# One expert layer of a deep kernel, dense over all experts, rewritten as a routed layer over tiles of slots

## The chip, the cores and the metric

The kernel runs on one core of a Trainium2 chip. The metric is the device time of one execution in microseconds, as the median over several runs. The kernel is one program that computes a network of four blocks, each an attention-like part and a feed-forward part; the change touches one of the eight parts, the feed-forward part of the third block.

## The reference

The part in question routes each of 2048 tokens (128 features) to one of 8 experts, an expert being two linear maps with 512 hidden features between them. In the reference all experts are computed for all tokens, and a mask keeps the chosen one:

```
B, S, D = (8, 1024, 128); H = 512; O = 128; E = 8; TOP_K = 1
xf = x.reshape(-1, d)
router_logits = xf @ Wr + br
topk_logits, topk_idx = jax.lax.top_k(router_logits, TOP_K)
topk_gates = jax.nn.softmax(topk_logits, axis=1)
for k in range(TOP_K):
    idx_k = topk_idx[:, k]
    gate_k = topk_gates[:, k:k + 1]
    for e in range(E):
        h = jax.nn.relu(xf @ W1[e] + b1[e])
        oe = h @ W2[e] + b2[e]
        mask = (idx_k == e)[:, None]
        out = out + jnp.where(mask, gate_k * oe, 0.0)
```

With one expert per token the softmax runs over one value, so the gate is 1. The layer's input is the normalised stream, and its output is added to the stream H.

## The kernel before

The program is written as a row of stages, each a block with one instruction stream per engine; a barrier of all engines closes a block. The part in question is called with the name "m2" and is made of five of them. `normalise` (m2n) writes XT, features by tokens. `route_softmax` (m2r) makes the logits (L229, L243), takes the largest (L246, L249), builds a gate per token and expert and stores the gates to DRAM; at the same time XT is split into a high and a low part (XR) and the weights of expert 0 are split on GpSimd (L379, L381). `relu_experts` (m2x) is the expert stage; `add_turned` (m2a) turns the result back and adds it to H (L169, L177). The same functions serve another layer, m1, with 16 experts.

Every product is made of three matmuls of reduced-precision parts (`product`, L306 to L308): high x high, low x high, high x low. So each factor must be split first. In `relu_experts` a step s is one expert e, one group g of 512 tokens, and one chunk c of 128 of the 512 hidden features: 8 x 4 x 4 = 128 steps. Per step TensorE makes the first product (`first`, into one of four PSUM banks `ph`) and, three steps behind it (LAG), the second (`second`, summed over the four chunks into `py`). ScalarE applies the relu with bias (L493) and, for even steps, makes the high part HS (L500); VectorE makes the high part of odd steps (L528), the low part of all (L532), and the gating and adding per group (L540, L549). The weights of the next expert are rounded by ScalarE (L506) and their low part is made by VectorE (L553), once in 16 steps. SyncE loads weights and gate rows, an expert or more ahead.

Two other places of the program matter for reading the change. `choose_tokens` gathers 2048 rows of 512 bytes from DRAM in 16 indirect DMAs on GpSimd, each with one row number per partition (L1247). `route_grouped` counts tokens per expert in a chain of 15 dependent additions (L997).

The order of the work on each engine is the order in which it is written; nothing reorders it, and a wait holds up all that stands behind it on its engine or queue.

## Time and profile before

| | us |
|---|---|
| median of 3 runs | 3247.32 |
| lowest and highest run | 3238.9, 3250.64 |
| the profiled execution, its own time | 3243.43 |
| its span, first to last instruction | 3241.6 |
| TensorE busy (share of the span) | 2544.6 (78%) |
| VectorE busy | 2352.4 (73%) |
| ScalarE busy | 1327.5 (41%) |
| GpSimd busy | 1419.5 (44%) |
| mean granted TensorE clock | 0.892 |

The rows are of that one execution. The busy shares are averages over stages with different limits, so for one stage they say little. Times within the trace are counted from the first instruction; the m2 part fills the stretch from about 2621 to 2854 us.

### The profile page before, as it was taken

The numbers are of one execution on the slowest core, as the hardware profiler recorded it, in microseconds if no ns is written. First come the engines' busy times: TensorE is split into PE (matmuls) and PEld (weight loads), VectorE is DVE, ScalarE is ACT, GpSimd is POOL, SyncE is SP. The second block draws the span as 40 slices with busy tenths as digits, with TensorE's granted clock in tenths as the row PEclk, the third lists the DMA queues.
The fourth block names the chain that finished last, engine by engine and source line by source line (L and its number), as shares of the span: only waits on it lengthen the run. The fifth ranks groups of instructions, "written<-read, shape, count | busy, mean of one in ns | idle before, by whom it ended". The sixth has DMA issues, their size and how long they took to land. (4 is left out here: it accounts for less than half of the span.)

```text
span 3241.6 us, 29207 instructions
## 1 busy us (share of the span) xinstructions
PE 2544.6 (78%) x8955; PEld 1510.7 (47%) x8955; DVE 2352.4 (73%) x3437; ACT 1327.5 (41%) x2109; POOL 1419.5 (44%) x897
## 2 busy tenths in 40 slices
PE   1778777677787772999857979479999659969599
PEld 0323222332332331666534837357777437733366
DVE  5699799759988976555557485658888548859566
ACT  2644444254454431222253343147776326730222
POOL 1499789649978971111123516110000310017266
PEclk9899889889999985999878989779999859979799
DMA  5155065116505410565300000022120011100021
GB/s 138 34 121 115 13 131 111 36 23 127 118 23 119 105 54 17 134 139 139 92 17 10 17 0 0 5 74 76 62 79 27 6 53 63 43 12 18 12 81 65
DMA packets 86604, 203.35 MB, mean 63 GB/s; under 512 B 12816, under 2 KB 25184, under 8 KB 77920
## 3 DMA queue, kind: packets, MB, share of 16 engines
q1 hardware_dynamic: 85952, 200.63, 24.6%
q8 instruction: 64, 1.05, 0.1%
q0 software_dynamic: 512, 1.05, 0.1%
q14 instruction: 76, 0.62, 0.1%
HBM read 198.76 MB, written 2.88 MB: 62 GB/s over the span
## 5 line engine op out<-in xcount | busy, mean ns | idle before, releaser
L532 DVE TENSOR_TENSOR m1x_HS<-m1x_R,m1x_HS 128x512 fp32r<-128x512 f32 x256 | 175.8, 691 | 69.2 <-ACT m1x_HS L500 64.9
L493 ACT ACTIVATE m1x_R<-m1x_ph,m1s_W 128x512 f32<-128x512 f32 x256 | 176.3, 689 | 107.2 <-PE m1x_ph L308 106.5
L1337 POOL TENSOR_TENSOR t2x_KM<-t2x_KT,t2x_HM 128x2048 f32<-128x2048 f32 x8 | 28.8, 3603 | 432.7 <-ACT t2x_KT L1410 416.0
L1688 POOL TENSOR_TENSOR t3xs_QH<-t3xs_HS,t3xa_Q 128x512 f32<-128x512 f32 x64 | 81.0, 1266 | 287.9 <-DVE t3xs_HS L1672 287.9
L829 DVE TENSOR_TENSOR m0x_T<-m0x_S,m0x_pb 128x512 f32<-128x512 f32 x128 | 88.1, 689 | 131.3 <-PE m0x_pb L308 131.2
L815 ACT ACTIVATE m0x_S<-m0x_pa 128x512 f32<-128x512 f32 x128 | 76.5, 598 | 214.2 <-PE m0x_pa L308 214.2
L2117 PE MATMUL t0x1fs_acc<-t0x1fs_HC,g_ident 128*128 128x512 f32 x256 | 133.6, 654 | 38.6 <-POOL t0x1fs_HC L2198 38.5
L2117 PE MATMUL t0x0fs_acc<-t0x0fs_HC,g_ident 128*128 128x512 f32 x256 | 133.2, 651 | 38.3 <-POOL t0x0fs_HC L2198 38.2
L2117 PE MATMUL t0x1bs_acc<-t0x1bs_HC,g_ident 128*128 128x512 f32 x256 | 131.2, 641 | 39.3 <-POOL t0x1bs_HC L2198 39.2
L2117 PE MATMUL t0x0bs_acc<-t0x0bs_HC,g_ident 128*128 128x512 f32 x256 | 130.2, 639 | 35.7 <-POOL t0x0bs_HC L2198 35.6
L2198 POOL TENSOR_TENSOR t0x1bs_HC<-t0x1bs_HS,t0x1bs_CB 128x1024 f32<-128x1024 f32 x64 | 149.1, 2360 | 10.7 <-DMA t0x1bs_CB<-t0x1b_bc_rows 4.2
L2198 POOL TENSOR_TENSOR t0x0bs_HC<-t0x0bs_HS,t0x0bs_CB 128x1024 f32<-128x1024 f32 x64 | 149.2, 2363 | 10.0 <-DMA t0x0bs_CB<-t0x0b_bc_rows 3.8
L2198 POOL TENSOR_TENSOR t0x1fs_HC<-t0x1fs_HS,t0x1fs_CB 128x1024 f32<-128x1024 f32 x64 | 148.5, 2343 | 7.0 <-DMA t0x1fs_CB<-t0x1f_bc_rows 5.2
L2198 POOL TENSOR_TENSOR t0x0fs_HC<-t0x0fs_HS,t0x0fs_CB 128x1024 f32<-128x1024 f32 x64 | 148.7, 2350 | 5.4 <-DMA t0x0fs_CB<-t0x0f_bc_rows 4.0
L332 POOL TENSOR_TENSOR m0s_WR<-m0s_W,m0s_ZERO 128x256 fp32r<-128x256 f32 x32 | 26.8, 838 | 259.6 <-DMA m0s_W<-in_L_units 259.4
L794 PE MATMUL m0x_acc<-m0x_HF,m0s_W 128*128 128x512 f32 x256 | 131.5, 595 | 3.8 <-DVE m0x_HF L838 3.8
L532 DVE TENSOR_TENSOR m2x_HS<-m2x_R,m2x_HS 128x512 fp32r<-128x512 f32 x128 | 88.0, 692 | 44.0 <-ACT m2x_HS L500 41.8
L493 ACT ACTIVATE m2x_R<-m2x_ph,m2s_W 128x512 f32<-128x512 f32 x128 | 88.2, 689 | 54.0 <-PE m2x_ph L308 53.6
L634 POOL TENSOR_TENSOR m3x_HF<-m3x_T,m3x_GS 128x512 f32<-128x512 f32 x64 | 81.7, 1280 | 58.0 <-DVE m3x_T L706 55.7
L306 PE MATMUL m1x_py<-m1x_HS,m1s_WR 128*128 128x512 f32 x256 | 103.3, 403 | 1.4 <-DVE m1x_HS L532 1.3
L306 PE MATMUL m0x_pa<-m0s_XR,m0s_WR 128*128 128x512 f32 x128 | 101.8, 795 | 1.8 <-PEq L890 1.8
L306 PE MATMUL m1x_ph<-m1s_XR,m1s_WR 128*128 128x512 f32 x256 | 102.3, 400 | 0.0
(915 smaller groups left out, 7637.6 us busy)
## 6 DMA issues: line engine op xcount, KB each, us to landing
m0x_GS<-m_gate_rows SPq DMA_DIRECT2D x64, 512.0 KB, 6.6
t0x0fs_CB<-t0x0f_bc_rows SPq DMA_DIRECT2D x32, 512.0 KB, 6.3
t0x0bs_CB<-t0x0b_bc_rows SPq DMA_DIRECT2D x32, 512.0 KB, 6.5
t0x1fs_CB<-t0x1f_bc_rows SPq DMA_DIRECT2D x32, 512.0 KB, 6.4
t0x1bs_CB<-t0x1b_bc_rows SPq DMA_DIRECT2D x32, 512.0 KB, 6.6
m1x_GS<-m_gate_rows SPq DMA_DIRECT2D x16, 1024.0 KB, 4.7
m1s_W<-in_L_w SPq DMA_DIRECT2D x16, 514.0 KB, 3.3
m2x_GS<-m_gate_rows SPq DMA_DIRECT2D x8, 1024.0 KB, 4.7
```

Of the source, the lines that this page charges most:

```text
L306: pe.matmul(out, lhsT[0], rhs[0], start=start, stop=False, skip_group_check=True)
L332: pool.tensor_tensor(self.WR[:, j, 0, :], self.W[:, j, 0:self.cut], self.ZERO[:, :], ALU.add).then_inc(self.rounded, 1)
L493: a.activation(R[:, s % 4, :], ph[s % 4][:, :], ACT.Relu, bias=W[:, e % RAW, weights.cut + c:weights.cut + c + 1]).then_inc(relu_ready, 1)
L532: v.tensor_tensor(HS[:, s % 4, 1, :], R[:, s % 4, :], HS[:, s % 4, 0, :].bitcast(F32), ALU.subtract).then_inc(low_made, 1)
L634: nc.gpsimd.tensor_tensor(HF[:, s % 3, :], T2[:, s % 2, :], GS[:, u // 2 % 2, tokens(g)], ALU.mult).then_inc(gated, 1)
L794: pe.matmul(acc[g][:, :], W[:, u % RAW, 2 * P:3 * P], HF[:, s % 3, :], start=(u == 0), stop=(u == UNITS - 1), skip_group_check=True).then_ ...
L815: nc.scalar.activation(S[:, s % 2, :], pa[s % 2][:, :], ACT.Silu).then_inc(s_ready, 1)
L829: v.tensor_tensor(T2[:, s % 2, :], S[:, s % 2, :], pb[s % 2][:, :], ALU.mult).then_inc(t_ready, 1)
L1337: nc.gpsimd.tensor_tensor(KM[:, i % 2, :, :], keys, spread(HM[:, :], W), ALU.mult).then_inc(km_made, 1)
L1688: nc.gpsimd.tensor_tensor(QH[:, s % 4, :], HS[:, s % 4, :], Q[:, c], ALU.mult).then_inc(read, 1)
L2117: mm = pe.matmul(acc[:, dh, :], ident[:, :], HC[:, m % 3, dh, :], start=False, stop=False, skip_group_check=True)
L2198: nc.gpsimd.tensor_tensor(HC[:, m % 3, :, :], HS[:, m % 5, :, :], rows, ALU.mult).then_inc(hc_made, 1)
```

## The change

The call of `relu_layer` for m2 is replaced by two new functions. `route_sparse` finds each token's expert and gives it a slot: the tokens of an expert stand one after another, each expert's slots begin at a multiple of 512, and 11 tiles of 512 slots hold every possible distribution. The 16 tiles of normalised rows are scattered into a DRAM array of 11 x 512 rows, cleared before. `sparse_experts` then works on the tiles: it loads 512 rows, turns them on TensorE, splits them (high part on ScalarE, low part on VectorE), runs 4 chunks as before, adds the second bias, turns the result back, and stores it. At the end GpSimd gathers each token's row, and VectorE multiplies by the gate and adds it to H. The weights of a tile's expert are gathered by row number, four tiles' worth up front; the later ones by GpSimd between its splits of the low parts, which it now makes. The first bias and the second stand in the weight rows (1029 columns). All 11 tiles are computed, full or empty. The router's matmuls and the normalisation stay as they were.

```
+def route_sparse(nc, name, XT, XN, ident, iota, earlier, pick, w_router, b_router, w12, E, out):
...
+            @block.sync
+            def _(sp):
+                sp.dma_start(wr[:, :], w_router[:, :]).then_inc(loaded, 16)
+                sp.dma_start(br[:, :], b_router.partition_broadcast(P)).then_inc(loaded, 16)
+                sp.wait_ge(blanked, 1)
+                for q in range(GROUPS):
+                    part = slot_rows[q * P * NT:(q + 1) * P * NT, :].rearrange("(p a) d -> p (a d)", a=NT)
+                    sp.dma_start(part, blank[:, :]).then_inc(cleared, 16)
...
+            @block.vector
...
+                for t in range(1, TILES):
+                    link(v.tensor_tensor(ahead[:, t, :], ahead[:, t - 1, :], inall[:, t - 1, :], ALU.add))
...
+            @block.gpsimd
+            def _(pool):
+                nc.gpsimd.memset(blank[:, :], 0.0).then_inc(blanked, 1)
+                pool.wait_ge(weight_row_ready, 1)
+                for j in range(len(w_loaded)):
+                    pool.indirect_dma_start(W[:, j, :], None, w12,
+                                            bass.IndirectOffsetOnAxis(ap=weight_row[:, j:j + 1], axis=0)).then_inc(w_loaded[j], 16)
+                pool.wait_ge(slot_ready, 1)
+                pool.wait_ge(cleared, 16 * GROUPS)
+                for t in range(TILES):
+                    pool.indirect_dma_start(slot_rows, bass.IndirectOffsetOnAxis(ap=slot[:, t:t + 1], axis=0),
+                                            XN[:, t, :], None).then_inc(scattered, 16)
...
+def sparse_experts(nc, name, H, ident, w12, out_rows, r):
...
+            @block.sync
+            def _(sp):
+                sp.wait_ge(scattered, 16 * TILES)
+                for j in range(3):
+                    sp.dma_start(XG[:, j, :, :], rows(slot_rows, j)).then_inc(x_loaded[j], 16)
+                for j in range(NT):
+                    sp.wait_ge(yt_read, j + 1)
+                    sp.dma_start(rows(out_rows, j), YT[:, j % 2, :, :]).then_inc(y_stored[j % 2], 16)
+                    if j + 3 < NT:
+                        sp.wait_ge(x_turned, j + 1)
+                        sp.dma_start(XG[:, j % 3, :, :], rows(slot_rows, j + 3)).then_inc(x_loaded[j % 3], 16)
...
+            @block.tensor
...
+                for s in range(STEPS):
+                    j, c = s // C, s % C
+                    if c == 0 and j + 1 < NT:
+                        turn_in(j + 1)
+                    if s + LAG < STEPS:
+                        first(s + LAG)
+                    second(s)
+                    if c == 1 and j:
+                        turn_out(j - 1)
+                turn_out(NT - 1)
...
+            @block.scalar
...
+                def round_w(j):
+                    act.wait_ge(w_loaded[j % RAW], 16 * (j // RAW + 1))
+                    if j >= 2:
+                        act.wait_ge(summed, (j - 1) * C)
+                    a.activation(WR[:, j % 2, 0, :], W[:, j % RAW, 0:CUT], ACT.Copy).then_inc(w_high, 1)
...
+                round_x(0)
+                for s in range(STEPS + 1):
+                    j, c = s // C, s % C
+                    if s < STEPS:
+                        relu(s)
+                    if s and (s - 1) % 2 == 0:
+                        high(s - 1)
+                    if s < STEPS and c == 0 and j + 1 < NT:
+                        round_w(j + 1)
+                        round_x(j + 1)
+                    if c == 3 and j:
+                        read(j - 1)
+                read(NT - 1)
...
+            @block.vector
...
+                split_x(0)
+                for s in range(STEPS):
+                    j, c = s // C, s % C
+                    low(s)
+                    if c == 0 and j + 1 < NT:
+                        split_x(j + 1)
+                    if c == 3 and j:
+                        copy_y(j - 1)
...
-        relu_layer("m2", 8, 1, "L2_ffn_Wr", "L2_ffn_br", "L2_w12", "L2_ffn_b2")
+        with Stage(nc, "m2s") as s:
+            NT, E = 11, 8
+            XN = s.sb("XN", [P, TILES, P])
+            normalise(nc, "m2n", H, XT, ident, XN)
...
+            route_sparse(nc, "m2r", XT, XN, ident, iota, consts["earlier"], consts["pick"], ins["L2_ffn_Wr"],
+                         ins["L2_ffn_br"], ins["L2_w12"], E, r)
+            sparse_experts(nc, "m2x", H, ident, ins["L2_w12"], out_rows, r)
```

ScalarE's row in the expert stage before, where the first chunks are followed by the rounding of the next expert's weights (R is the relu's output, HS the high part, WR the split weights, OT the sum):

```order
L510 ACTIVATE m2s_OT<-m2x_py 128x512 x4
L493 ACTIVATE m2x_R<-m2x_ph,m2s_W 128x512 x2
L500 ACTIVATE m2x_HS<-m2x_R 128x512
L493 ACTIVATE m2x_R<-m2x_ph,m2s_W 128x512 x2
L500 ACTIVATE m2x_HS<-m2x_R 128x512
L493 ACTIVATE m2x_R<-m2x_ph,m2s_W 128x512 x2
L500 ACTIVATE m2x_HS<-m2x_R 128x512
L493 ACTIVATE m2x_R<-m2x_ph,m2s_W 128x512
L506 ACTIVATE m2s_WR<-m2s_W 128x1024
```

The same engine in the changed program, one tile from its first relu to the next tile's (XR is the split x, Y the second product with its bias):

```order
L863 ACTIVATE m2x_R<-m2x_ph,m2s_W 128x512
L850 ACTIVATE m2s_WR<-m2s_W 128x1024
L856 ACTIVATE m2x_XR<-m2x_px 128x512
L863 ACTIVATE m2x_R<-m2x_ph,m2s_W 128x512
L870 ACTIVATE m2x_HS<-m2x_R 128x512
L863 ACTIVATE m2x_R<-m2x_ph,m2s_W 128x512 x2
L870 ACTIVATE m2x_HS<-m2x_R 128x512
L876 ACTIVATE m2x_Y<-m2x_py,m2s_W 128x512
L863 ACTIVATE m2x_R<-m2x_ph,m2s_W 128x512
```

The rounding of weights stood once in 16 steps; now it stands once in 4, with the rounding of x behind it, both between a tile's first relu and the first high part.

SyncE's queue before, through the m2 stages (GS are the gate rows, W the weights):

```order
L212 DMA m2r_wr<-in_L_ffn_Wr 128x8
L213 DMA m2r_br<-in_L_ffn_br 128x8
L369 DMA m2s_W<-in_L_w 128x1028 x3
L218 DMA m_gate_rows<-m2s_gateF 8x512 x4
L434 DMA m2x_B<-in_L_ffn_b 8x128
L439 DMA m2x_GS<-m_gate_rows 128x2048
L369 DMA m2s_W<-in_L_w 128x1028
```

and in the changed program (XG are the loaded rows of a tile, YT the turned result):

```order
L622 DMA m2r_wr<-in_L_ffn_Wr 128x8
L623 DMA m2r_br<-in_L_ffn_br 128x8
L627 DMA m_slot_rows<-m2r_blank 128x1408 x4
L764 DMA m2x_XG<-m_slot_rows 128x512 x3
L767 DMA m_out_rows<-m2x_YT 128x512
L770 DMA m2x_XG<-m_slot_rows 128x512
L767 DMA m_out_rows<-m2x_YT 128x512
```

The weights have left this queue, and each load of x now stands behind a store.

GpSimd before did the first splits and was then idle until the next block; in the changed program it issues the indirect DMAs (slot holds a row number per token, weight_row one per partition and tile):

```order
L705 MEMSET m2r_blank 128x1408
L708 DMA m2s_W<-in_L_w,m2s_weight_row 128x1029 x4
L713 DMA m_slot_rows<-m2s_XN,m2s_slot 5632x128 x16
L776 TENSOR_TENSOR m2s_WR<-m2s_W,m2s_WR 128x1024 x2
L782 DMA m2s_W<-in_L_w,m2s_weight_row 128x1029
L776 TENSOR_TENSOR m2s_WR<-m2s_W,m2s_WR 128x1024
```

After the last tile another 16 indirect DMAs (L788) gather the results.

## Rows read from the trace of the kernel before

**Rows 1.** Windows: the expert stage; us, busy us (instructions) per engine, clock, DMA

```profile
core 0: us, PE busy (x) PEld busy (x) DVE busy (x) ACT busy (x) POOL busy (x), PEclk, DMA share, GB/s
2662.00:2848.00 186.00, 183.98 (x768) 144.46 (x768) 154.72 (x262) 127.95 (x200) 0.00 (x0) 0.99 0.13 46
```

**Rows 2.** Waits in 2664 to 2848: who for whom, us in total, times, longest

```profile
ACT m2x_R L493 <- PE m2x_ph L308: 53.6, 113, 1.0
...
PEld m2x_py L306 <- DVE m2x_HS L532: 7.3, 16, 1.1
```

**Rows 3.** Timeline, routing of m2: start us, duration us, engine, line, operation

```profile
2642.03 0.29 DVE L243 TENSOR_TENSOR m2r_logits<-m2r_pl,m2r_br 128x128 f32<-128x128 f32 x1 [10.51 <-PE m2r_pl L229]
...
2645.88 0.23 DVE L251 CAST m2r_wheref<-m2r_where 128x128 f32<-128x128 uint32 x1
```

**Rows 4.** Timeline, end of m2

```profile
2849.13 3.65 PE L169 MATMUL m2a_turned<-g_ident,m2s_OT 128*128 128x128 f32 x16 [1.77 <-PEq L431]
...
2852.82 0.69 DVE L177 TENSOR_TENSOR g_H<-g_H,m2a_turned 128x512 f32<-128x512 f32 x1 [0.16 <-PE m2a_turned L169]
```

**Rows 5.** Timeline, the counting chain of layer m0

```profile
1282.34 3.80 DVE L997 TENSOR_TENSOR m0r_ahead<-m0r_ahead,m0r_inall 128x64 f32<-128x64 f32 x15
```

**Rows 6.** Timeline, the gathers of choose_tokens, first and last of 16

```profile
43.14 0.17 DVE L1228 CAST tok_index<-tok_spreadrows 128x16 uint32<-128x16 f32 x1 [0.70 <-PE tok_spreadrows L1240]
43.61 1.15 POOL L1247 DMA_INDIRECT g_H<-in_x,tok_index  x1 [43.19 <-DVE tok_index L1228]
...
62.54 0.94 POOL L1247 DMA_INDIRECT g_H<-in_x,tok_index  x1 [0.30 <-issue]
65.19 0.87 DVE L1232 BATCH_NORM_STATS2 t0m_stats<-g_H 128x6 f32<-128x128 f32 x4 [4.19 <-DMA g_H<-in_x,tok_index]
```

**Rows 7.** DMA issues: count, KB each, us from issue to landing

```profile
m1s_W<-in_L_w SPq DMA_DIRECT2D x16, 514.0 KB, 3.3
...
t0x0fs_BB<-t0x0f_bc_rows SPq DMA_DIRECT2D x21, 256.0 KB, 3.6
...
g_H<-in_x,tok_index POOLq DMA_INDIRECT x16, 2.5
t0x0i_WI<-in_L_attn_in SPq DMA_DIRECT2D x1, 256.0 KB, 2.5
...
t0x0b_bc_rows<-t0x0bp_BCF SPq DMA_DIRECT2D x1, 256.0 KB, 2.6
```

**Rows 8.** Groups by line, 2621 to 2866: busy us, mean ns, idle before

```profile
L506 ACT ACTIVATE m2s_WR<-m2s_W 128x1024 fp32r<-128x1024 f32 x7 | 7.4, 1056 | 0.0
...
L147 ACT ACTIVATE g_XT<-m2n_turned 128x512 f32<-128x512 f32 x4 | 2.4, 598 | 3.1 <-PE m2n_turned L154 3.1
...
L381 POOL TENSOR_TENSOR m2s_WR<-m2s_W,m2s_WR 128x1024 fp32r<-128x1024 f32 x1 | 2.3, 2342 | 0.1
```

**Rows 9.** Timeline, first products of the expert stage

```profile
2663.77 0.63 PE L307 MATMUL m2x_ph<-m2s_XR,m2s_WR 128*128 128x512 f32 x1
...
2664.20 0.63 PE L308 MATMUL m2x_ph<-m2s_XR,m2s_WR 128*128 128x512 f32 x1
```

**Rows 10.** Timeline, near the stage's end: VectorE, then ScalarE

```profile
2841.21 0.69 DVE L532 TENSOR_TENSOR m2x_HS<-m2x_R,m2x_HS 128x512 fp32r<-128x512 f32 x1 [0.42 <-ACT m2x_HS L500]
2841.82 0.42 DVE L528 TENSOR_SCALAR m2x_HS<-m2x_R 128x512 fp32r<-128x512 f32 x1
2842.27 0.69 DVE L532 TENSOR_TENSOR m2x_HS<-m2x_R,m2x_HS 128x512 fp32r<-128x512 f32 x1
...
2842.75 0.69 ACT L493 ACTIVATE m2x_R<-m2x_ph,m2s_W 128x512 f32<-128x512 f32 x1 [0.70 <-PE m2x_ph L308]
2843.34 0.62 ACT L500 ACTIVATE m2x_HS<-m2x_R 128x512 fp32r<-128x512 f32 x1
```

**Rows 11.** Windows of 2 us in the scan layer; columns as in rows 1

```profile
444.00:446.00 2.00, 0.16 (x1) 0.00 (x0) 2.00 (x2) 1.31 (x2) 2.00 (x1) 1.00 0.39 83
...
454.00:456.00 2.00, 0.37 (x1) 0.38 (x2) 2.00 (x2) 1.13 (x3) 2.00 (x2) 0.89 0.50 156
456.00:458.00 2.00, 2.00 (x3) 0.80 (x3) 1.97 (x2) 1.20 (x2) 2.00 (x2) 0.50 0.94 137
```

More of the change, by code:

```diff
@@ L2902, in build @@
         recycle(nc)
-        relu_layer("m2", 8, 1, "L2_ffn_Wr", "L2_ffn_br", "L2_w12", "L2_ffn_b2")
+        with Stage(nc, "m2s") as s:
+            NT, E = 11, 8
+            XN = s.sb("XN", [P, TILES, P])
+            normalise(nc, "m2n", H, XT, ident, XN)
+            r = dict(tiles=NT, gate=s.sb("gate", [P, TILES]), slot=s.sb("slot", [P, TILES], U32),
+                     weight_row=s.sb("weight_row", [P, NT], U32), W=s.sb("W", [P, 4, ins["L2_w12"].shape[-1]]),
+                     WR=s.sb("WR", [P, 2, 2, 8 * P], F32R), w_high=s.sem("w_high"), w_split=s.sem("w_split"),
+                     w_loaded=[s.sem(f"w_loaded{j}") for j in range(4)], scattered=s.sem("scattered"),
+                     slot_rows=nc.dram_tensor("m2_slot_rows", (NT * GROUP, P), F32, kind="Internal").ap())
+            out_rows = nc.dram_tensor("m2_out_rows", (NT * GROUP, P), F32, kind="Internal").ap()
+            route_sparse(nc, "m2r", XT, XN, ident, iota, consts["earlier"], consts["pick"], ins["L2_ffn_Wr"],
+                         ins["L2_ffn_br"], ins["L2_w12"], E, r)
+            sparse_experts(nc, "m2x", H, ident, ins["L2_w12"], out_rows, r)
         recycle(nc)
@@ L2932, in lay_out @@
     d = {"x": a["x"]}
-    for n in ("L1_ffn_router_w", "L1_ffn_router_b", "L1_ffn_b2", "L2_ffn_Wr", "L2_ffn_br", "L2_ffn_b2"):
+    for n in ("L1_ffn_router_w", "L1_ffn_router_b", "L1_ffn_b2", "L2_ffn_Wr", "L2_ffn_br"):
         d[n] = a[n]
@@ L2939, in lay_out @@
                                         b1.reshape(E, 4, P).transpose(0, 2, 1)], axis=2)
+    d["L2_w12"] = np.concatenate([d["L2_w12"], a["L2_ffn_b2"][:, :, None]], axis=2).reshape(8 * P, -1)
     d["L0_tok_W"], d["L0_tok_b"] = a["L0_tok_W"], a["L0_tok_b"]
@@ L2949, in lay_out @@
     d["c_pick"] = np.concatenate([blocks % 8 == np.arange(8), blocks // 8 == np.arange(TILES), blocks * P,
-                                  np.zeros((P, TILES - 1))], axis=1).astype(np.float32)
+                                  blocks, np.zeros((P, TILES - 2))], axis=1).astype(np.float32)
     m = {n: a["L0_attn_" + n] for n in ("in_proj_w", "conv_w", "conv_b", "xproj_w", "dtproj_w", "dtproj_b", "A_log",
```

250 lines of the change are left out of this document (added).

## The prediction

> **What bounds the kernel now.** I read three views. The whole program is long and only the layer called m2 changes, so I cut that out with the windows view. From 2662 to 2848 us TensorE is busy 184.0 of 186 us at a granted clock of 0.99, with VectorE at 154.7 and ScalarE at 128.0 [rows 1]: the expert stage runs at TensorE's pace. The waits say the same: ScalarE waits 53.6 us for TensorE's products, TensorE's weight port only 7.3 us for VectorE [rows 2]. The same window gives the pace: 768 matmuls of 512 columns in 186 us, 0.24 us each; six of them make a step (3 for the first layer, 3 for the second), so 1.4 us, and 128 steps make the 180 us. The routing ahead of it starts its VectorE part at 2642.03 [rows 3], and the last addition to H ends at 2852.82 + 0.69 = 2853.51 [rows 4]. What precedes 2642.03 (normalise, router weights, router matmuls) and what follows 2853.51 is the same in both programs. So the sum is made on one stretch: 211.5 us now.
>
> **The change, part by part.** It replaces 8 experts x 4 groups x 4 chunks = 128 steps by 11 tiles x 4 = 44 steps. It adds a slot computation on VectorE, 4 weight gathers and 16 scatters on GpSimd, a trip through DRAM for the rows, per tile two turns on TensorE and an x split, and 16 gathers at the end. At TensorE's pace alone 84 steps less would save 118 us. I walk the new path instead.
>
> *1. Slot computation.* The same 3.9 us from the logits to the cast of the indices [rows 3], then the chosen mask (about 0.3) and two matmuls (0.5). Then 15 chained additions: the same loop in layer m0 takes 3.80 us for 15 of 64 columns [rows 5], 0.25 each; with 8 columns I take 0.2, 2.9 in all. Ten more small links of 0.2 to 0.28 give the weight rows. Sum 9.8: 2651.8. The slots are 2 us later, behind the weight gathers, so they cost nothing.
>
> *2. GpSimd's indirect DMAs.* The trace has 16 gathers of the same shape (128 rows of 512 B): 43.61 for the first, 62.54 for the last, 15 starts later, so 1.26 us each; the last data is used at 65.19, 2.65 after its issue [rows 6], and the landing is given as 2.5 [rows 7]. Here 4 weight gathers (rows of 4.1 KB) and 16 scatters stand in one row: 0.3 to start (43.31 to 43.61 there) + 19 x 1.25 + 2.5 = 26.6: the rows lie in DRAM at 2678.4. The clearing of the slots (four stores, 2.9 MB) is queued over 20 us ahead of the first scatter, and 0.5 MB lands in 3.3 [rows 7]: hidden. No row shows a scatter or a gather of 4.1 KB rows; below, I take no less than 1.25, above twice that, and choose 1.25 since the count of rows is the same.
>
> *3. Fill.* Load of x 2.8 (256 KB: 2.5 alone, 3.6 beside others [rows 7]), turn at half clock 1.1 (16 of them take 3.65 [rows 4]), rounding 0.65 [rows 8], subtraction 0.75, then three first products at half clock of 1.28 each (0.43 x 3 [rows 9]) = 9.2: 2687.6, where the turn for tile 1 begins. Neither the 26.6 nor the 9.2 has a counterpart now.
>
> *4. One middle tile, from the moment L at which its next x has landed.* An engine starts its next instruction about 0.1 before the last one's reported end: ScalarE 0.59 after a relu of 0.69; VectorE 0.61 after a subtraction of 0.69, 0.45 after a cast of 0.42 [rows 10]. ScalarE's order is fixed: relu, round w (1.06 [rows 8]), round x, relu, high, relu, relu, high, read. Turn in to L+0.5; round x 0.55 to 1.15; relu from 1.05; high 1.65 to 2.27; VectorE: low 2.3, x subtraction 2.9, cast 3.5, low 3.95, low 4.6, cast 5.2, low 5.65, and only then the copy of the turned y, 6.25 to 6.9. TensorE meanwhile turns, does one first product (to 1.2), **waits for the low part until 3.05**, and ends the tile's eighth product at L+8.7. Its own work is 24 x 0.24 + 8 turns (1.0) = 6.8, so about 2 us of idleness per tile come from ScalarE's queue: the high part of the very chunk that TensorE wants stands behind round w and round x. The weight split on GpSimd (2.34 [rows 8]) ends by about L+3.5, ahead of its use at 3.75.
>
> *5. Who waits behind the store.* SyncE's order is: wait for the copied y of tile j, store it, and only then issue the load of x for tile j+3. The copy that comes at L+6.9 therefore releases the x that is wanted at L+8.7. Store issue 0.5, load landing 2.5 (alone) to 3.6 (beside other traffic) [rows 7]; I take 3.3, since a 256 KB store is right ahead of it. That is L+10.7: x is late by 2 us, and the loop copy, store, load, turn, copy sets the period, not TensorE. It holds for x 3 to 10.
>
> *6. Clock.* Per tile TensorE now has two gaps of about 2 us. Rows of the scan layer: after a gap of the same kind at 444 the clock stayed at 1.00; after the one at 454 it fell to 0.50 [rows 11]. So gaps of this length stand at the border between the two levels (1.2 and 2.4 GHz). I add 0.3 us per tile as a mean: period 11.0.
> The Trainium skill, TensorE: Matmul & The Clock Gate, section "HAM oscillation — how this bites in real kernels", speaks against this change: waits between short bursts take the clock down each time, so that every burst begins at half rate. By that rule every tile pays; by the row at 444 none does. What this would be is a rival below, worked out from rows.
>
> *7. Sum.* 2687.6; tile 0 without load stall or turn out 8.4: 2696.0; tile 1 10.7; tiles 2 to 8 7 x 11.0 = 77.0; tile 9 without a load to wait for at its end 8.7; tile 10 has no rounding in front of it and runs at TensorE's pace, 4.2: 2796.6. Read, turn out, copy 2.0; store 2.6 [rows 7]: 2801.2. Gathers 0.3 + 15 x 1.25 + 2.5 = 21.5; four additions of 0.35 with little overlap 1.3: **2824.0**. Against 2853.5 that is 29.5 us less. The profiled execution took 3243.4 us by its own time (span 3241.6), so 3213.9; the median of the runs is 3.9 above it: **3218**.
>
> **Weights.** The gather of tile n is issued once the y that used its buffer is read, about 15 us before the rounding wants it; 514 KB land in 3.3 [rows 7]. Hidden with 10 us to spare; if it were not, each of 7 tiles would pay its lateness.
>
> **The rivals.**
> *A, x is not late (0.15).* If store and load do not disturb each other and the copy comes earlier than walked, the period is that of step 4 with the weight rounding starting at the tile's beginning, about 9.1. For it: WI landed in 2.5. Against: even 2.5 gives L+9.9. Gain 29.5 + 8 x 1.9 = 45: 3203.
> *B, TensorE's pace holds (0.05).* 6.8 us per tile: tiles 1 to 8 save about 4.2 more each and tiles 0 and 9 about 1.7, gain 29.5 + 37 = 66: 3181. Against it stands ScalarE's order.
> *C, half clock in every tile (0.18).* First and second products cost 1.28 instead of 0.70. Between L and the copy lie the turn, two seconds, one first and the turn out: these push the copy from 6.9 to 9.3, the period from 10.7 to 13.1, 2.1 above the one in the sum. Gain 29.5 - 8 x 2.1 - 4 for the other tiles = 9: 3239. For it: two gaps with one short burst between them come close to what stood ahead of the fall at 454 [rows 11]. Against: the rest of the tile is one long burst.
> *D, slower than before (dearer DMAs 0.12, of which 0.07 dear enough to lose).* 36 indirect DMAs are on the path, each with GpSimd's issue time. At 1.25 they cost 45 us of the 182 that the new path takes. From 1.25 + 29.5/36 = 2.07 us each the change loses; at 2.5, twice the row, it is 3218 + 36 x 1.25 = 3263. For it: a scatter writes DRAM and the weight rows are 8 times longer; against: the time is per row index, and all 16 seen cost the same 1.25 but the first. The Trainium skill, DMA: Bandwidth & Descriptors, section "Bandwidth", advises batches of 1 MiB and calls transfers under 64 KB descriptor-bound, which these 32 transfers are at the edge of.
> *E, no effect.* Not possible: 84 of 128 steps do go.
>
> **From this to the numbers.** Forecast 0.50, A 0.15, B 0.05, C 0.18, D 0.12. About 0.5% (16 us) is what this measurement can tell from no change; the bound for faster is 3231. Forecast, A, B and a quarter of C are beyond it: 0.75. The rest of C and a part of D lie within: 0.18; slower 0.07. Range 3198 to 3242: A and C nearly whole, a quarter of D; left out are B, the rest of D and the edges, 0.18.
>
> **What would show it.** Right: indirect DMAs 1.25 us apart, about 49 us from the logits to the first second-layer product; TensorE waiting for VectorE's low part about 2 us once per tile; the x turn waiting for a DMA 1 to 2.5 us at 8 tiles; last slots gathered 22 us after the last store. Wrong: periods under 9.5 (A, B), a clock of 0.8 or less in the expert stretch with products of 1.28 (C), spacings above 1.6 on GpSimd (D). The largest single risk is the period, counted ten times.

## The result, and the profile of the changed kernel

The changed kernel takes 3227.4 us (median of 7 runs, 3223.9 to 3237.3), the kernel before 3241.2 (7 runs, 3238.0 to 3250.6): a ratio of 0.9956, 95% interval 0.9939 to 0.9973. The forecast was 3218 with 3198 to 3242 around it. The profiled execution took 3224.4 us, with a span of 3222.6 against 3241.6.

The stretch on which the sum was made, from the logits to the last addition to H, ends at 2832.63 + 1.14 and began at 2642.32: 191.5 us, where 182.0 was forecast and 211.5 stood before. The rest of the program differs by some microseconds from run to run (the stretch begins between 2638.3 and 2647.5 us in the profiled executions below), so the experiments are compared on this stretch and on the period of a tile, and the medians stand beside them.

The timeline of the changed kernel follows, its columns as in [rows 3]: the slot computation, the gathers and scatters, the first load of x; then one whole tile; then the end.

```profile
2642.32 0.29 DVE L658 TENSOR_TENSOR m2r_logits<-m2r_pl,m2r_br 128x128 f32<-128x128 f32 x1 [8.89 <-PE m2r_pl L633]
2647.37 2.90 DVE L675 TENSOR_TENSOR m2r_ahead<-m2r_ahead,m2r_inall 128x8 f32<-128x8 f32 x15
2652.20 0.17 DVE L686 CAST m2s_weight_row<-m2r_expert 128x11 uint32<-128x11 f32 x1
2652.65 1.04 POOL L708 DMA_INDIRECT m2s_W<-in_L_w,m2s_weight_row  x1 [19.24 <-DVE m2s_weight_row L686]
2657.73 1.01 POOL L713 DMA_INDIRECT m_slot_rows<-m2s_XN,m2s_slot  x1 [0.30 <-issue]
...
2677.08 0.97 POOL L713 DMA_INDIRECT m_slot_rows<-m2s_XN,m2s_slot  x1 [0.30 <-issue]
2680.42 1.27 SPq L764 DMA_DIRECT2D m2x_XG<-m_slot_rows  x3
...
2720.46 1.06 ACT L850 ACTIVATE m2s_WR<-m2s_W 128x1024 fp32r<-128x1024 f32 x1 [3.35 <-PE m2x_py L308]
2721.59 2.36 POOL L776 TENSOR_TENSOR m2s_WR<-m2s_W,m2s_WR 128x1024 fp32r<-128x1024 f32 x1 [4.81 <-ACT m2s_WR L850]
2721.85 0.66 PE L799 MATMUL m2x_px<-g_ident,m2x_XG 128*128 128x128 f32 x4 [1.49 <-DMA m2x_XG<-m_slot_rows]
2724.27 0.69 DVE L911 TENSOR_TENSOR m2x_HS<-m2x_R,m2x_HS 128x512 fp32r<-128x512 f32 x1 [5.93 <-ACT m2x_HS L870]
2725.11 0.47 PE L306 MATMUL m2x_py<-m2x_HS,m2s_WR 128*128 128x512 f32 x1 [1.91 <-DVE m2x_HS L911]
2727.27 1.12 POOL L782 DMA_INDIRECT m2s_W<-in_L_w,m2s_weight_row  x1 [3.31 <-ACT m2x_Y L876]
2728.21 0.68 DVE L918 COPY m2x_YT<-m2x_pt 128x512 f32<-128x512 f32 x1
2728.92 0.32 SPq L767 DMA_DIRECT2D m_out_rows<-m2x_YT  x1
2729.28 0.43 SPq L770 DMA_DIRECT2D m2x_XG<-m_slot_rows  x1
2733.32 0.97 PE L799 MATMUL m2x_px<-g_ident,m2x_XG 128*128 128x128 f32 x4 [2.47 <-DMA m2x_XG<-m_slot_rows]
...
2811.37 0.96 POOL L788 DMA_INDIRECT m2x_YG<-m_out_rows,m2s_slot  x1 [16.27 <-DMA m_out_rows<-m2x_YT]
2832.63 1.14 DVE L932 SCALAR_TENSOR_TENSOR g_H<-m2x_YG,m2s_gate,g_H 128x128 f32<-128x128 f32 x4 [3.79 <-DMA m2x_YG<-m_out_rows,m2s_slot]
```

The middle group shows one loop. The x turn is at 2721.85, TensorE's stop for the low part ends at 2725.11, the copy of the turned y at 2728.21, its store at 2728.92, the load behind it at 2729.28, and the next turn waits 2.47 us for a DMA and comes at 2733.32. The waits of TensorE from 2697.7 to 2793.3 (columns as in [rows 2]) show the same two stops per tile; before, the largest stop was the weight port's for VectorE, 7.3 us in 184 [rows 2]:

```profile
PEld m2x_py L306 <- issue: 15.9, 7, 2.3
PE m2x_py L306 <- DVE m2x_HS L911: 15.5, 8, 2.7
PEld m2x_px L799 <- DMA m2x_XG<-m_slot_rows: 14.8, 8, 2.9
PE m2x_px L799 <- DMA m2x_XG<-m_slot_rows: 11.5, 8, 2.5
```

The windows view, one line per period from turn to turn, then all eight (columns as in [rows 1]):

```profile
2697.73:2710.23 12.50, 8.44 (x34) 6.19 (x32) 4.96 (x8) 6.64 (x10) 3.20 (x3) 0.86 0.27 84
2710.23:2721.85 11.62, 8.23 (x32) 6.18 (x33) 4.64 (x8) 5.70 (x9) 3.21 (x3) 0.85 0.29 93
2721.85:2733.32 11.47, 7.10 (x33) 5.05 (x33) 4.55 (x8) 5.70 (x9) 4.46 (x3) 1.00 0.29 92
2733.32:2745.18 11.86, 9.34 (x32) 6.89 (x32) 4.64 (x8) 5.70 (x9) 2.21 (x2) 0.71 0.26 89
...
2697.73:2793.22 95.49, 68.55 (x257) 51.04 (x256) 37.37 (x64) 46.52 (x73) 25.27 (x16) 0.82 0.26 83
```

TensorE is busy 68.6 of 95.5 us at a clock of 0.82; before it was busy all the time at 0.99 [rows 1]. Only one of the eight periods ran at full clock, and it is hardly shorter (11.47) than the others: this is the odd thing that the experiments had to explain.

The landings in the DMA part of the profile (the median of each group, in microseconds from issue) answer to [rows 7]:

```profile
m_slot_rows<-m2r_blank SPq DMA_DIRECT2D x4, 704.0 KB, 6.0
m2x_XG<-m_slot_rows SPq DMA_DIRECT2D x11, 256.0 KB, 3.1
m_out_rows<-m2x_YT SPq DMA_DIRECT2D x11, 256.0 KB, 2.0
m_slot_rows<-m2s_XN,m2s_slot POOLq DMA_INDIRECT x16, 2.2
m2x_YG<-m_out_rows,m2s_slot POOLq DMA_INDIRECT x16, 2.5
m2s_W<-in_L_w,m2s_weight_row POOLq DMA_INDIRECT x11, 4.3
```

### The profile page after: what moved, and what is told of

Its sections match the earlier page's. It is cut to its first block and busy times, and to the rows that moved or that the text cites. A ratio compares the mean times of both kernels' runs of the same rounds, so it can differ in the third digit from the quotient of the medians.

```text
span 3222.6 us, 27930 instructions
## 1 busy us (share of the span) xinstructions
PE 2437.5 (76%) x8501; PEld 1428.4 (44%) x8501; DVE 2255.8 (70%) x3306; ACT 1256.3 (39%) x2000; POOL 1473.2 (46%) x947
## 5 line engine op out<-in xcount | busy, mean ns | idle before, releaser
L2565 POOL TENSOR_TENSOR t0x1bs_HC<-t0x1bs_HS,t0x1bs_CB 128x1024 f32<-128x1024 f32 x64 | 149.1, 2356 | 10.7 <-DMA t0x1bs_CB<-t0x1b_bc_rows 4.2
L306 PE MATMUL m1x_ph<-m1s_XR,m1s_WR 128*128 128x512 f32 x256 | 102.2, 399 | 0.0
L307 PE MATMUL m1x_ph<-m1s_XR,m1s_WR 128*128 128x512 f32 x256 | 102.1, 399 | 0.0
L308 PE MATMUL m1x_ph<-m1s_XR,m1s_WR 128*128 128x512 f32 x256 | 101.5, 396 | 0.0
```

What stands on the lines that cost most here:

```text
L306: pe.matmul(out, lhsT[0], rhs[0], start=start, stop=False, skip_group_check=True)
L307: pe.matmul(out, lhsT[1], rhs[0], start=False, stop=False, skip_group_check=True)
L308: return pe.matmul(out, lhsT[0], rhs[1], start=False, stop=stop, skip_group_check=True)
L2565: nc.gpsimd.tensor_tensor(HC[:, m % 3, :, :], HS[:, m % 5, :, :], rows, ALU.mult).then_inc(hc_made, 1)
```

## The experiments

Period is the time from one x turn to the next, as a mean over the seven periods from the turn of x 3 to that of x 10, and the clock is the mean over them. The kernel before had medians of 3241.1 to 3242.8 beside them. The ratios are an estimate over all runs and not the quotient of the medians (for x_all_ahead that would be 0.9942), so kernels that lie close are told apart by the stretch. With the changed kernel first:

| kernel | median us | ratio to before, 95% | stretch | period | clock in it |
|---|---|---|---|---|---|
| changed kernel | 3227.4 | 0.9956 (0.9939 to 0.9973) | 191.5 | 11.86 | 0.81 |
| w_gather_later | 3227.7 (one run) | | 191.3 | 11.94 | 0.80 |
| x_all_ahead | 3224.1 | 0.9925 (0.9902 to 0.9948) | 188.2 | 11.07 | 0.85 |
| pe_filler | 3225.6 | 0.9941 (0.9921 to 0.9961) | 192.1 | 11.84 | 0.96 |
| w_rounded_earlier | 3233.4 | 0.9961 (0.9940 to 0.9981) | 198.5 | 12.49 | 0.77 |
| w_gather_behind_x | 3237.5 | 0.9991 (0.9981 to 1.0001) | 207.2 | 13.64 | 0.75 |
| filler_w_behind_x | 3234.9 | 0.9983 (0.9973 to 0.9993) | 203.8 | 13.67 | 0.88 |
| w_gather_behind_split | 3227.7 | 0.9939 (0.9917 to 0.9962) | 193.0 | 12.01 | 0.78 |
| filler_w_behind_split | 3216.7 | 0.9923 (0.9907 to 0.9940) | 180.2 | 10.35 | 1.00 |
| x_ahead_split_vector | 3225.3 | 0.9954 (0.9939 to 0.9968) | 190.7 | 11.26 | 0.89 |
| x_ahead_w_earlier | 3214.8 | 0.9927 (0.9911 to 0.9944) | 180.9 | 10.41 | 0.84 |
| all_hoisted_w_later | 3185.7 | 0.9822 (0.9808 to 0.9837) | 152.0 | 7.52 | 0.97 |
| all_hoisted_vector | 3181.1 | 0.9812 (0.9797 to 0.9827) | 145.4 | 6.73 | 1.00 |

**GpSimd's indirect DMAs: w_gather_later.** Two of the four weight gathers ahead of the scatters are issued behind them instead.

```
-                for j in range(len(w_loaded)):      # route_sparse, ahead of the scatters
+                for j in range(2):
...
+                for j in range(2, RAW):             # sparse_experts, ahead of the splits
+                    pool.indirect_dma_start(W[:, j, :], None, w12, ...).then_inc(w_loaded[j], 16)
```

> As the changed kernel, but only two of the four weight gathers stand ahead of the scatters; the other two are issued at the start of the expert stage. If GpSimd's issue is what the scatters wait for, as in the sum: 2 x 1.25 = 2.5 us from the last weight row to the first load of x less, 25.6 instead of 28.05. Rival (the scatters' landing is held up by transfers, clearing or weights): no change.

From the first weight gather to the first load of x it was 25.0 us (2655.61 to 2680.62) instead of 27.8 (2652.65 to 2680.42): 2.8 us less for two DMAs, with 2.5 expected. GpSimd's issue time is what sets this part. Behind it 2.6 of them were lost again, 1.5 of these behind the last turn of x; why is not shown.

**Is the late x the bound: x_all_ahead and w_rounded_earlier.** The first loads all 11 tiles before the first tile; the second keeps x by tile and rounds the weights two tiles ahead.

```
-                for j in range(3):                  # x_all_ahead, SyncE
+                for j in range(NT):
                     sp.dma_start(XG[:, j, :, :], rows(slot_rows, j)).then_inc(x_loaded[j], 16)
```

```
                     if s < STEPS and c == 0 and j + 1 < NT:      # w_rounded_earlier, ScalarE
-                        round_w(j + 1)
                         round_x(j + 1)
+                    if s < STEPS and c == 2 and j + 2 < NT:
+                        round_w(j + 2)              # WR has three buffers instead of two
```

> All 11 loads of x are issued up front into 11 buffers, so none stands behind a store; nothing else differs from the changed kernel, whose tiles start 11.85 us apart. My theory (the store and the load behind it close the loop): the waits of the turn for x disappear after the first; ScalarE's rounding of w then delays that of x by 0.5, so tiles start 9.1 us apart at full clock and about 9.8 if the clock still falls in some of them; 8 tiles x 2.0 to 2.7 = 16 to 22 us less than the changed kernel, a span near 3204. Rival (the clock alone makes the tiles long): the period stays above 11.3 and the span above 3218.

> As the changed kernel, but with three buffers of split weights, and ScalarE rounds the weights of tile j+2 in the middle of tile j instead of those of tile j+1 at its start. My theory (the late x decides): in tiles 1 to 8 the rounding of w was over before x was turned, so nothing changes there; 0 to 2 us less in all, period 11.8. Rival (ScalarE's queue, rounding of w ahead of the high part, is what the tiles wait for): 1 us per tile, 10 us less.

With x ahead, the waits for x are gone, and the stretch is 3.3 us shorter, where 16 to 22 were expected: the period is 10.0 in tiles at full clock and up to 12.4 where the clock falls. The wait that remains, for VectorE's low part, had grown to 3.14 us in the tile shown here (1.91 in the tile of the changed kernel above). The timeline of x_all_ahead shows a part of the reason: the low part took 1.36 instead of 0.69, and GpSimd's split of the weights ran beside it.

```profile
2727.68 2.34 POOL L773 TENSOR_TENSOR m2s_WR<-m2s_W,m2s_WR 128x1024 fp32r<-128x1024 f32 x1 [5.11 <-ACT m2s_WR L847]
2729.21 1.36 DVE L908 TENSOR_TENSOR m2x_HS<-m2x_R,m2x_HS 128x512 fp32r<-128x512 f32 x1 [4.80 <-ACT m2x_HS L867]
```

With the weights earlier and x by tile, nothing was gained, as expected while x is late. It even lost 7 us, and that was not expected. Of these, 4.4 lie in the seven periods: the clock fell to 0.77, and both parts of the loop are longer, 8.9 us from turn to store (8.4 in the changed kernel) and 3.6 from store to turn (3.5). Another 1.6 lie ahead of them, where GpSimd's split has moved beside two low parts of tile 1 that take 3.06 us together instead of 1.29, and 1.2 behind them.

**Is it the clock: pe_filler.** TensorE does products that nobody reads in both gaps: six while it waits for x, and the one first product of the tile's start three times over.

```
                     if c == 0 and j + 1 < NT:
+                        if j >= 2:
+                            pe.wait_ge(x_split, j + 1)
+                            for i in range(6):
+                                pe.matmul(px[:, :], WR[:, j % 2, 0, 0:P], XR[:, j % 2, 0, :], ...)
                         turn_in(j + 1)
                     if s + LAG < STEPS:
-                        first(s + LAG)
+                        first(s + LAG, 3 if c == 0 and j + 1 < NT else 1)
```

> As the changed kernel, but TensorE fills its two gaps per tile with repeated products that change no result: 6 matmuls into the empty turn bank before it waits for x (from tile 2 on), and the first product of the tile's last chunk three times instead of once. It does 12 matmuls more per tile, 2.9 us at full clock. My theory (the half clock costs 1.3 to 2 us per tile because turn out and copy come late): granted clock above 0.95 in the expert stretch instead of 0.84, copy 7.0 us after the turn instead of 8.8, tiles 10.5 apart instead of 11.85, 8 to 12 us less. Rival (the half clock falls into waiting time and costs nothing): no change or, since the work is more, up to 3 us more.

The clock rose to 0.96, and the period stayed at 11.84, where 10.5 was expected. The timeline of pe_filler, one tile:

```profile
2726.79 0.66 PE L799 MATMUL m2x_px<-g_ident,m2x_XG 128*128 128x128 f32 x4 [1.30 <-DMA m2x_XG<-m_slot_rows]
2732.20 1.12 POOL L782 DMA_INDIRECT m2s_W<-in_L_w,m2s_weight_row  x1 [4.49 <-ACT m2x_Y L883]
2733.85 0.32 SPq L767 DMA_DIRECT2D m_out_rows<-m2x_YT  x1
2738.16 0.66 PE L799 MATMUL m2x_px<-g_ident,m2x_XG 128*128 128x128 f32 x4 [1.04 <-DMA m2x_XG<-m_slot_rows]
```

Turn to store is 7.06 us here, where the prediction walked to 6.9. But store to turn is 4.31 here and 4.9 in the mean of the seven tiles in which a weight gather (514 KB) is issued 1.1 to 1.9 us ahead of the store; in the eighth, without one, it is 3.13 (2794.89 to 2798.02). The changed kernel's one tile at full clock has the same 4.4 us; in its others the store comes 2.7 us or more behind the gather, and store to turn is 3.2 to 3.6. This suggests that the lower clock and the weight gather hide each other; the next four kernels test it.

**Is it the weight gather: w_gather_behind_x and filler_w_behind_x.** GpSimd holds the gather until the next x has been turned; the second has the filler too.

```
                         pool.wait_ge(y_read, n - RAW + 1)
+                        pool.wait_ge(x_turned, j + 2)
                         pool.indirect_dma_start(W[:, n % RAW, :], None, w12, ...
```

> The changed kernel, with GpSimd's weight gather held until the next x has been turned. It tests a second thing that could make x late. In the three profiled kernels that still load x by tile, the turn of x starts 5.8 to 7.5 us after the weight gather's issue, wherever the store stands. Theory 'x queues behind the 514 KB weight gather': without it each x is turned 3.1 to 3.3 us after the store, as in the one tile of the changed kernel that has no gather ahead of it (2789.89 to 2793.22). The changed kernel has 3.2 to 3.5 in six tiles and 4.4 in one, so the gain is small, 1 to 3 us in all: stretch 189 to 190.5, mean period 11.6, about 3225. Theory 'the load's own landing and the clock decide': nothing changes, stretch 191 to 192. Slower, above 193, if the gather behind the turn disturbs the store of the tile or comes late for the rounding (it has about 6 us less than before out of 15).

> pe_filler (TensorE kept busy in both gaps by matmuls that nobody reads) together with the weight gather behind the x turn. In pe_filler the clock rose to 0.97 but the period stayed at 11.84, since from store to x turn it was 4.3 to 5.6 us where a weight gather stood 1.4 to 2 us ahead of the store, and 3.13 in the one tile without. Theory 'x queues behind the weight gather': store to turn 3.2 in every tile, turn to store 7.1 at full clock, period 10.3 to 10.6, stretch 180 to 183 (pe_filler 192.1), about 3216: this is the clock term of the changed kernel, freed from the transfer that had hidden its worth. Theory 'the filler itself slows the x load or the copy': store to turn stays above 4, period 11.5 to 12, stretch 190 or more.

Without a gather ahead of it, x was turned 2.97 to 3.35 us after each store in w_gather_behind_x. With the filler it was 3.35 to 3.66, but there the turn follows the filler at once, so x may have landed earlier; the first one, 4.35, had a load that took 1.63 us to issue instead of 0.43, and why is not shown. But both kernels were slower, by 16 and 12 us in the stretch. The timeline of w_gather_behind_x:

```profile
2727.11 3.00 DVE L912 TENSOR_TENSOR m2x_HS<-m2x_R,m2x_HS 128x512 fp32r<-128x512 f32 x1 [5.42 <-ACT m2x_HS L871]
2727.19 2.36 POOL L776 TENSOR_TENSOR m2s_WR<-m2s_W,m2s_WR 128x1024 fp32r<-128x1024 f32 x1
2730.03 0.68 DVE L900 TENSOR_TENSOR m2x_XR<-m2x_px,m2x_XR 128x512 fp32r<-128x512 f32 x1
```

The held gather had pushed GpSimd's split to just where VectorE makes the low part for which TensorE waits: 3.00 us instead of 0.69. The difference, 2.31, is the length of the split, 2.36. The expectation had overlooked that the wait stands ahead of the next split in GpSimd's order.

**Both causes apart: w_gather_behind_split and filler_w_behind_split.** The gather is issued right behind GpSimd's split, 4.7 to 7.0 us ahead of the store; the second adds the filler.

```
-                    n = j + RAW - 2
+                    n = j + RAW - 3
```

> w_gather_behind_x showed that x lands 3.0 to 3.35 us after the store when no weight gather stands ahead of it, but it pushed GpSimd's split onto VectorE's low part (0.69 to 3.00 us), which made it slower. Here the gather is issued directly behind GpSimd's split, about 5 us ahead of the store, so that it meets neither. Otherwise the changed kernel as it is. Theory: store to turn 3.1 in every tile, low parts 0.69, turn to store as the clock has it (7.1 at full clock, 8.7 to 9.1 where it falls): period 10.2 in tiles at full clock, 11.8 to 12.1 in the others, mean 11.3 to 11.7, stretch 187 to 191. Rival 'the gather's landing costs nothing': as the changed kernel, 11.86 and 191.5 within a microsecond. Slower if the gather's issue holds VectorE up.

> w_gather_behind_split with the filler matmuls of pe_filler, which nobody reads. The difference between the two is the price of the clock with no transfer in the way, the term that the prediction put at 0.3 us per tile. Theory: granted clock 0.97, turn to store 7.1, store to turn 3.1, period 10.2 to 10.4, stretch 178 to 182, so the clock's price is 1.2 to 1.5 us per tile. Rival 'the clock is worth little': period less than 0.5 us below w_gather_behind_split's. Rival 'the filler holds the transfers or VectorE up': store to turn above 4 again.

The windows view over seven periods, of w_gather_behind_split, then of filler_w_behind_split:

```profile
2712.71:2796.77 84.06, 63.16 (x224) 47.35 (x225) 33.35 (x56) 39.59 (x63) 23.46 (x14) 0.78 0.28 88
```

```profile
2709.63:2782.08 72.45, 68.42 (x308) 51.15 (x308) 32.23 (x56) 39.93 (x63) 22.86 (x15) 1.00 0.32 102
```

The second does more work on TensorE and takes 11.6 us less for seven tiles: 12.01 - 10.35 = 1.66 us per tile is the price of the clock. All of it lies between turn and store, 7.1 us in the mean instead of 8.8; store to turn is 3.2 in both (in the second the turn follows the filler at once, so 10.35 may be a little above what x alone would allow). Moving the gather alone gained nothing (12.01 against 11.86), raising the clock alone gained nothing (11.84), both together gained 1.5 us per tile. With both, the stretch is 180.2 and the median 3216.7, close to the forecast's 182.0 and 3218, which had 0.3 us per tile in it for the clock and nothing for the gather.

**GpSimd's split and VectorE: x_ahead_split_vector.** x_all_ahead, with the weights' low part made by VectorE.

```
                     low(s)
                     if c == 0 and j + 1 < NT:
+                        dve.wait_ge(w_high, j + 2)
+                        v.tensor_tensor(WR[:, (j + 1) % 2, 1, :], W[:, (j + 1) % RAW, 0:CUT], ..., ALU.subtract)
                         split_x(j + 1)
```

> x_all_ahead (all 11 loads of x before the first tile) with the low part of the weights made by VectorE, ahead of its x subtraction, instead of by GpSimd. It tests whether VectorE's low part is stretched by GpSimd's split: in x_all_ahead the low part for which TensorE waits took 1.36 us beside GpSimd's split (2.34) and 0.69 elsewhere, and TensorE waited 3.1 us. Theory 'the two engines hinder each other': each low part 0.69, the wait of TensorE 2.4, GpSimd's time is gone; VectorE's own split costs about 1.2 and stands where VectorE has time, so the period at full clock goes from 10.0 to 9.3 and the mean from 11.07 to about 10.4: stretch 181 to 183. Rival 'the long low part has its cause elsewhere' (operands, bank of the accumulator): low stays 1.36, VectorE has 1.2 more, stretch 188 or more.

Every low part took 0.69 again, so the long one did come from GpSimd. TensorE's wait for it went from 3.14 to 2.48 us. The time was not won, though: TensorE now waited 0.76 more for the split on VectorE, and the period is 11.26, where 10.4 was expected (10.5 in tiles at full clock, 10.0 before).

**ScalarE's order: x_ahead_w_earlier.** The two edits of the second group together.

> x_all_ahead together with the rounding of the weights two tiles ahead (three WR buffers), at chunk 2 instead of chunk 0. ScalarE's high part, for which TensorE waits through VectorE's low part, then stands behind the rounding of x alone (0.6), and GpSimd's split falls beside other low parts. w_rounded_earlier with x by tile brought nothing (period 12.49), which the theory 'the late x decides' foretold; with x ahead the same edit must pay. Theory: wait for the low part 3.1 to 1.0 to 1.4, period 8.2 to 9.2 (x_all_ahead 11.07), stretch 163 to 172 (x_all_ahead 188.1), about 3200. Rival 'not ScalarE's order but the clock sets the pace' : period 10.5 or more, stretch above 182.

Windows of four periods, then two lines of its timeline:

```profile
2696.98:2705.83 8.85, 7.04 (x34) 5.05 (x33) 4.64 (x8) 5.47 (x9) 2.47 (x2) 1.00 0.06 12
2705.83:2714.67 8.84, 6.94 (x34) 5.06 (x33) 4.64 (x8) 5.47 (x9) 3.23 (x3) 1.00 0.27 92
2714.67:2724.92 10.25, 8.34 (x34) 6.31 (x33) 4.74 (x8) 5.47 (x9) 4.82 (x3) 0.83 0.37 117
2724.92:2735.19 10.27, 8.37 (x33) 6.30 (x32) 4.74 (x8) 5.47 (x9) 3.27 (x2) 0.83 0.26 80
```

```profile
2732.23 0.69 DVE L917 COPY m2x_YT<-m2x_pt 128x512 f32<-128x512 f32 x1 [0.57 <-PE m2x_pt L822]
2732.50 2.01 POOL L773 TENSOR_TENSOR m2s_WR<-m2s_W,m2s_WR 128x1024 fp32r<-128x1024 f32 x1
```

The edit that lost 7 us while x was late brings 7.2 once it is not. TensorE's one stop is down to 1.90 us: of the 3.14 in x_all_ahead 0.66 were GpSimd's hold on VectorE and 0.58 the rounding of the weights ahead of that of x. In the timeline the split now stands beside the copy of y, which still takes 0.69. Two periods ran at full clock, 8.85 us; the next five, 10.2 to 10.3, pay 1.4 for a clock of 0.83 with the same stop. The last, 12.8, has two low parts beside the split again (3.06 us instead of 1.29). So the theory's 8.2 to 9.2 held for two periods, and the rival had the rest.

**A version from all this: all_hoisted_w_later and all_hoisted_vector.** x_ahead_w_earlier and w_gather_later, five raw weight buffers, and the turn half a tile earlier; the second makes the weights' low part on VectorE at the end of a tile.

```
-                    if c == 0 and j + 1 < NT:
-                        turn_in(j + 1)
+                    if s == 0:
+                        turn_in(1)
+                    if c == 2 and j + 2 < NT:
+                        turn_in(j + 2)
```

```
                     if c == 3 and j:
                         copy_y(j - 1)
+                    if c == 3 and j + 2 < NT:       # all_hoisted_vector, VectorE
+                        split_w(j + 2)
```

> A version made from what the runs showed: all loads of x before the first tile, weights rounded two tiles ahead, five raw weight buffers, only two weight gathers ahead of the scatters, and, new, the turn of the next x at chunk 2 of the tile before instead of at the tile's start. x_ahead_w_earlier (stretch 180.9, period 10.25 at a granted clock of 0.87, 8.85 in its two quickest tiles) still lets TensorE wait 1.90 us once per tile, since the high part of the chunk that it wants is made only after the rounding of an x that was turned just before. Theory 'turn and rounding of x in one place cause the gap, and the gap the lower clock': with the turn half a tile earlier there is no gap, the clock stays above 0.95, and the period is TensorE's own work, 6.8 to 7.4 us; stretch about 180.9 - 10 x 3.1 - 2.5 for the gathers = 147, 143 to 155, about 3182. Rival 'GpSimd's split stretches VectorE': a low part beside the split took 3.0 us instead of 0.69 in w_gather_behind_x; VectorE then has up to 4.7 + 2.3 = 7.0 us per tile and the period is 7.5 to 8.5, stretch 158 to 168. Rival 'the clock falls for another reason': clock below 0.9 without gaps, period 8.5 or more.

> all_hoisted_w_later with the low part of the weights made by VectorE at the end of a tile instead of by GpSimd. If GpSimd's split stretches VectorE's work by as much as it lasts, this costs VectorE 1.2 us per tile and gives back up to 2.3: period 6.8 to 7.2 and 2 to 10 us less than all_hoisted_w_later. If VectorE has slack there anyway, the two are equal within 2 us; if VectorE's 1.2 us stand in the way of a low part, this one is slower by up to 10 us.

Both beat both kernels. The windows view of all_hoisted_vector, one period, then eight and 0.3 us of the next:

```profile
2692.34:2699.07 6.73, 6.57 (x34) 5.26 (x33) 5.64 (x11) 5.78 (x9) 0.00 (x0) 1.00 0.02 6
2692.34:2746.50 54.16, 52.85 (x260) 42.36 (x259) 46.35 (x74) 46.44 (x72) 7.35 (x6) 1.00 0.31 94
```

TensorE is busy 52.9 of 54.2 us at full clock: its own pace, 6.73 us per tile, where step 4 of the prediction had counted 6.8. Before the change the expert stage ran at TensorE's own pace too [rows 1]; now it has a third of the steps. With the split on GpSimd (all_hoisted_w_later) low parts of 1.2 to 1.6 us stand beside it in the first tiles, later two that take 3.34 us together, for which TensorE stops 2.0 us. The period is 6.75 to 7.15 us before that stop, as the theory had it, and 7.52 in the mean over all seven, where the rival of the stretched low part had 7.5 to 8.5. So moving the split to VectorE is worth 0.8 us per tile here, where x_ahead_split_vector had lost 0.2. There it stood ahead of the x split and TensorE stopped for it; here it is made before TensorE wants it, and no such wait is left.

## Why the prediction held, and where it was off

*Slot computation*: 9.8 forecast, 10.05 measured (2642.32 to 2652.37), the chain 2.9 and 2.90.

*GpSimd's indirect DMAs*: to the first load of x 28.1 instead of 26.6. The weight gathers start 1.24 to 1.35 apart, as in [rows 6]; the scatters 1.27 to 1.28, the first two 1.32 and 1.46, landing in 2.2. These starts make 0.7 of the 1.5. The other 0.8 lie behind the last start, 3.34 us from 2677.08 to the load at 2680.42: I had counted the landing alone, 2.5, and not the close of the block. Rival D is refuted: neither the longer rows nor writing to DRAM made an indirect DMA dearer to issue. From the last product to the last addition, with the store and the gathers between, it took 26.9 with a forecast of 27.4.

*Fill* and tile 0: 9.0 and 8.3, with 9.2 and 8.4 forecast.

*One middle tile*: turn to copy to store was walked to L + 6.9 and 0.5; at full clock the store is at L + 7.07. TensorE stands for the low part until L + 3.26 (2725.11; 3.05 forecast), 1.91 us. One reason given for it was wrong: the high part does not stand behind the rounding of the weights, which ran at 2720.46, while TensorE waited for x. It stands behind the turn, the rounding of x and a relu. So w_rounded_earlier could win nothing here, and x_ahead_w_earlier could, where x is not late. The walk's times already had the weights' rounding out of the way; only the reason given beside them had it in.

*Who waits behind the store*: x 3 to 10 are late, as forecast, by 1.0 to 2.5 us. x_all_ahead took the waits away, and w_rounded_earlier showed that with x late an earlier rounding wins nothing. Rivals A and B (x not late, TensorE's pace) did not happen in this kernel; B's pace and B's 3181 us are what all_hoisted_vector reached with the waits removed. That it is 3181 to the microsecond is luck, as this kernel also issues two gathers fewer ahead of the scatters, which B had not counted.

*Clock*: this is the term that was wrong in size. I took 0.3 us per tile from the two gaps of [rows 11]; it costs 1.66 by the pair of filler runs, and seven of the eight periods paid for it in part (0.71 to 0.86). Most of rival C's mechanism was therefore true, a half clock through a part of the tile, at 1.66 of its 2.4 us per tile; C's 3239 us were not reached, as its cost replaced the gather's instead of adding to it. The sign that I had set for C was half there: behind the stop for the low part, products started 0.43 us apart (2737.45, 2737.88), the spacing of half clock in [rows 9], but the clock over the eight periods was 0.82. By the Trainium skill, TensorE: Matmul & The Clock Gate, section "HAM oscillation — how this bites in real kernels", bursts between waits begin at half rate each time. This trace agrees in part: the burst behind the stop for the low part begins at half clock in six of the eight tiles (its first product takes 0.76 to 0.77 us instead of 0.47), the one behind the wait for x in one of eight. The waits here are shorter than in the example that the Trainium skill works through. Even so its rule was nearer than my mean of two rows.

*Weights*: "hidden with 10 us to spare" was right for the rounding that reads them and wrong for the x load that lands behind them: 1.2 to 2.5 us in each tile of pe_filler in which the store comes within 2 us of the gather, 0.7 to 1.2 in three such tiles of w_rounded_earlier. As the clock's delay keeps the store further away, the two do not add, and the 10.7 to 11.0 per tile came out as 11.86. That they did not add is luck, as the prediction had neither in this size: with 1.66 and 1.49 both paid on top of 10.35, the period would be 13.5 and the median about 3239 (an estimate from these runs), at the edge of the range.

*Sum*: against the 182.0 forecast the changed kernel has +0.3 for the slots, +1.5 for the indirect DMAs, -0.3 for fill and tile 0, +1.8 for tile 1 (12.5, its low part stretched to 1.01 by GpSimd's split), +6.0 for tiles 2 to 8 (83.0 instead of 77.0), +0.8 for tiles 9 and 10, and -0.5 for the end: +9.5. The stretch became 20.0 us shorter, 29.5 was forecast. The profiled executions are 19.0 us apart and the medians of seven runs 13.8: the profiled execution of the kernel before lies 2.2 us above its median, that of the changed kernel 3.0 below. From three runs I had put the median 3.9 above the profiled execution. For the changed kernel that nearly came true, for the one before it did not, so this term was right by luck.

Two things stay open: why w_rounded_earlier's clock fell below the changed kernel's (0.77 against 0.81), and what decides, at a stop of 1.9 us once per tile, that two tiles of x_ahead_w_earlier kept the full clock and the next ones did not.

## What to carry to other kernels

When one engine's stop has two possible causes, removing one of them may show nothing because the other takes its place: test them singly and together, and look at the interval that each edit should shorten, not at the total. In a loop over tiles, take out of the ring of store, load, turn and rounding whatever can be issued a tile earlier before shortening any of its members; here such moves took the gain of a change from 0.4% to 1.9%. And a transfer that is hidden for its own reader is still in the way of the next one's.

## What the hardware showed that I had not expected

In these traces a VectorE subtraction that reads two operands from SBUF waits out GpSimd's tensor operation beside it. The low part took 0.69 us alone, 1.36 with 0.81 us of the split beside it, and 3.00 with all of its 2.36. An operation with one of its operands in PSUM was not held up: in all_hoisted_w_later the subtraction for x lies wholly inside a split and takes its usual time, as the copy of y did above, beside the first 0.4 us of a split.

```profile
2682.86 2.37 POOL L777 TENSOR_TENSOR m2s_WR<-m2s_W,m2s_WR 128x1024 fp32r<-128x1024 f32 x1
2683.07 0.69 DVE L904 TENSOR_TENSOR m2x_XR<-m2x_px,m2x_XR 128x512 fp32r<-128x512 f32 x1 [23.00 <-ACT m2x_XR L859]
```

The Trainium skill, SBUF — State Buffer, section "SBUF: two separate sides", says so: the two engines share a pair of ports under an exclusive lock, in which a VectorE operation with two SBUF inputs takes part. The trace agrees, with the numbers above. The Trainium skill there also gives the ports to the operation that starts first; at 2727.11 in w_gather_behind_x the low part is shown 0.08 us ahead of the split, and it was the one that waited, so the shown starts do not decide this. The prediction had not reckoned with it, although its own walk put the split (to L + 3.5) over the low part at L + 2.3. In the changed kernel the late x hid that: the weights were rounded while TensorE waited, and the split was over at 2723.95, 0.3 us before the low part began.

An indirect DMA of 128 rows of 4.1 KB, issued ahead of the expert stage, costs GpSimd the same 0.94 to 1.04 us of issue as most of those of 128 rows of 512 B (0.94 to 1.16); in the tiles it takes 1.07 to 1.12 in the changed kernel and up to 1.46 in others. Its 514 KB land in 4.3 us, and a 256 KB load whose store was issued within 2 us of it came 0.7 to 2.5 us later than without.
